# Language-model tower in float32 on one core: parameters loaded as rows, weights held back, the square of the FP4 rounding on ScalarE, and new step lists

## The chip, the cores and the metric

The kernel runs on one core of one Trainium2 chip. The metric is the device time of one execution in microseconds (us). The engines are TensorE (PE in the profile, its weight loads PEld), VectorE (DVE), ScalarE (ACT), GpSimd (POOL) and SyncE (SP). Each engine runs its own list of instructions in order and waits on semaphores.

## What is computed

16 sequences of 256 token ids (4096 tokens) pass through three blocks in float32: an embedding with a projection, one RWKV layer, and a gated feed-forward block whose inputs and weights are rounded to FP4 in blocks of 16.

```python
h = (w0[ids] @ w1) * mask * 16                        # 512 -> 256
x = layernorm(h)                                      # RWKV layer, T = 256
a = ln1(x); ax = shift(a)
k, v, r = mix_k(a, ax) @ wk, mix_v(a, ax) @ wv, sigmoid(mix_r(a, ax) @ wr)
x = x + (r * wkv_scan(k, v, time_decay, time_first)) @ wo
b = ln2(x); bx = shift(b)
x = x + sigmoid(mix_r(b, bx) @ cwr) * (relu(mix_k(b, bx) @ cwk) ** 2 @ cwv)
h = h + x
c = layernorm(h)                                      # FP4 feed-forward, 704 wide
g, u = q(c) @ q(w_gate).T, q(c) @ q(w_up).T
h = h + q(silu(g) * u) @ q(w_down).T
# q: scale = max|block of 16| / 6, then round |x| / scale to 0, .5, 1, 1.5, 2, 3, 4, 6
```

## The kernel before

The tokens are cut into 8 chunks of 512 (four tiles of 128, two sequences). Each chunk passes three stages: `a` (gather of embedding rows by GpSimd, transpose, projection, layer norm, mixes, k, v, r, and the scans and exponentials of the wkv), `b` (output projection, second layer norm, channel mix with the squared ReLU), and `c` (third norm, quantisation, gate and up products, quantisation of the 704-wide product tile by tile, down product, store). Up to three chunks are in flight at once.

What runs when is written out by hand. `ORDER` holds for each engine one list of steps `(name, lag)`; `walk` goes through it once for each t and calls the step for chunk t - lag, where that chunk exists. Steps whose name begins with `w` prepare weights and run once, for chunk 0. So the order on an engine is fixed, and an instruction that waits holds everything behind it. Between engines there are semaphores that count up (`Signal`); the PSUM areas of each stage (`A_JOBS`, `B_JOBS`, `C_JOBS`) have two slots each, and TensorE may write a slot only when the job before last in it was emptied (`wait_free`).

The steps that matter here: `c_norm0/1` on VectorE quantise the normed input (512 columns, two tiles at once), `c_quant0` to `c_quant3` the product tile (704 columns), `w_quant0` to `w_quant2` the weights gate, up and down, in two halves. All call `quantise`, which has nine stages, each waiting for the one before. Stage 0 is the maximum of each block, 1 and 2 scale and reciprocal, 3 divides. Then a magic number rounds: stage 4 masks the exponent out of the value, 5 forms max(exponent, 1) times `MAGIC`, 6 adds it, 7 subtracts it, 8 multiplies by the scale. `w_turn` transposes a quantised weight on TensorE, ScalarE copies the high part, `w_split` on VectorE forms the low part; `w_key` does the same for `cwk` (a copy on ScalarE, a subtraction on VectorE). The gate, up and key products use float32r matmuls and are split in three: high by high, high by low, low by high (`up`, `key` on TensorE).

At the start, SyncE issues the loads of the ids and `tok_w1` and then all weights, wk, wv, wr, gate, up, down, cwk, wo, cwr, cwv. ScalarE issues eleven loads of the parameter vectors, one value per partition (`v.rearrange("(h p) -> p h")`), and waits for all before it forms exp(time_decay); VectorE waits for that before its first list step:

```python
            act.wait_ge(s_par, 16 * len(PARAMS))
            nc.scalar.activation(decay[:, 0], par[:, td, :], ACT.Exp).then_inc(s_exp, 1)
            ...
            dve.wait_ge(s_exp, 1)
            nc.vector.tensor_scalar(decay[:, 1], decay[:, 0], -1.0, None, ALU.mult).then_inc(s_decay, 1)
```

Lines of the profile: L349, L351, L353, L355 are stages 0 to 3 of `quantise`, L358 and L360 stages 4 and 5, L362, L364 and L366 stages 6 to 8. L917 is a mix on VectorE, L730 its part on ScalarE, L955 the scan for the running maximum, L942 and L984 the products and sums of the wkv, L776 its exponentials. L811 and L814 are the ReLU and the square of the keys, L845 the SiLU, L782 the norm of stage b, L803 the copy in `w_key`. On TensorE L487 transposes the gathered rows, L499 is the embedding product, L527 k, v and r, L536 the products of stage b and `b_out`, L562 the keys, L604 gate and up, L631 down.

## Time and profile before

| | |
|---|---|
| median of 3 runs | 795.42 us (795.3 to 796.78) |
| the profiled execution | 792.87 us, span 791.0 us |
| mean granted clock of TensorE | 0.962 of full speed |
| TensorE busy, 3310 matmuls | 705.7 us (89%) |
| TensorE weight loads | 566.1 us (72%) |
| VectorE busy | 651.3 us (82%) |
| ScalarE busy | 473.9 us (60%) |
| GpSimd busy | 155.9 us (20%) |
| DMA over the span | 19.33 MB, mean 24 GB/s |
| chain that ended last, by engine | VectorE 45%, TensorE 30%, ScalarE 11%, issue 10% |

The span runs from the first to the last instruction; the execution's own time is a little longer. Busy times are unions of an engine's instructions. Two matmuls in flight overlap, and their ends are modelled, so start-to-start distances tell more of them than their lengths. The chain is followed back from the last instruction, at each step to whatever released it.

### The profile page before, as it was taken

Reading aid. Unit: us, or ns where it says so; the run is one execution under the profiler, and the core shown is the slowest. Engines: PE = TensorE matmul, PEld = TensorE weight load, DVE = VectorE, ACT = ScalarE, POOL = GpSimd, SP = SyncE. Lnnn points to the kernel's source line nnn. Section 1 sums busy time; section 2 is a strip of 40 time slices with the busy share of each in tenths; the row PEclk is TensorE's granted clock in tenths of the full one; section 3 lists DMA queues with packets and bytes.
Section 4 is the critical chain, followed back from the end, with each engine's and each line's share of the span. In section 5 each row is a group of like instructions: output and inputs, shape, how many; then the busy total and the mean of one; then the engine's idle time right before and its main releaser. Section 6 shows DMA issues by size and latency. Waiting matters only on the chain.

```text
span 791.0 us, 9857 instructions
## 1 busy us (share of the span) xinstructions
PE 705.7 (89%) x3310; PEld 566.1 (72%) x3310; DVE 651.3 (82%) x1131; ACT 473.9 (60%) x834; POOL 155.9 (20%) x220
## 2 busy tenths in 40 slices
PE   2563779899999999999999999999999999699687
PEld 2431656688688867887788868886788778688575
DVE  2987497899799987899789979998889969982874
ACT  1239388568665668377756866676837684561110
POOL 2213230324023401331032402340232003100000
PEclk9867899999999999999999999999999999999978
DMA  8400000000010001000010101000100000000000
GB/s 198 165 27 14 14 27 0 28 1 28 0 41 14 28 1 38 17 1 28 14 41 1 29 0 41 14 28 0 41 15 1 1 14 14 1 0 15 14 0 27
DMA packets 14903, 19.33 MB, mean 24 GB/s; under 512 B 3942, under 2 KB 12294, under 8 KB 14854
## 3 DMA queue, kind: packets, MB, share of 16 engines
q1 hardware_dynamic: 9302, 10.31, 4.3%
q0 software_dynamic: 2560, 8.39, 3.5%
q8 instruction: 27, 0.44, 0.2%
q10 hardware_dynamic: 2992, 0.01, 0.2%
q14 instruction: 22, 0.18, 0.1%
HBM read 14.51 MB, written 4.19 MB: 24 GB/s over the span
## 4 chain that ended last, share of the span: by engine, by line
DVE 45%; PE 30%; ACT 11%; issue 10%; DMA 2%; POOL 2%; DVEq 0%; ACTq 0%; POOLq 0%
PE psB L536 16%; PE psC L631 6%; DVE mix L917 5%; DVE top L349 4%; DVE hq L362 3%; DVE hq L364 3%; DVE hq L355 3%; DVE hq L1096 3%; DVE magic L360 2%; DVE magic L358 2%; DVE top L353 2%; DMA rows<-L_tok_w,ids_now 2%; ACT take L776 2%; PE psB L562 2%; PE psC L604 2%
## 5 line engine op out<-in xcount | busy, mean ns | idle before, releaser
L536 PE MATMUL psB<-cwv_s,kkT 128*128 128x256 f32 x512 | 113.9, 380 | 2.6 <-ACT kkT L814 2.6
L536 PEld LDWEIGHTS psB<-cwv_s,kkT 128*128 128x128 f32 x512 | 96.0, 190 | 20.8 <-ACT kkT L814 8.4
L527 PE MATMUL psA<-mix,kvr_s 128*128 128x512 f32 x192 | 91.4, 622 | 12.8 <-DVE mix L917 10.5
L604 PE MATMUL psC<-up_hi,xq_hi 128*128 128x352 f32 x256 | 89.8, 351 | 13.0 <-DVE xq_lo L1144 12.7
L631 PE MATMUL psC<-downT,hqT 128*128 128x256 f32 (+1 forms) x384 | 95.9, 395 | 0.0
L424 POOL DMA_INDIRECT rows<-L_tok_w,ids_now x32 | 38.6, 1207 | 270.1 <-PE psA L487 258.5
L631 PEld LDWEIGHTS psC<-downT,hqT 128*128 128x128 f32 (+1 forms) x384 | 69.6, 191 | 23.8 <-issue 15.9
L604 PE MATMUL psC<-up_lo,xq_hi 128*128 128x352 f32 x256 | 84.3, 329 | 0.0
L604 PE MATMUL psC<-up_hi,xq_lo 128*128 128x352 f32 x256 | 84.1, 328 | 0.0
L527 PEld LDWEIGHTS psA<-mix,kvr_s 128*128 128x128 f32 x192 | 36.7, 198 | 54.0 <-issue 40.8
L604 PEld LDWEIGHTS psC<-up_hi,xq_hi 128*128 128x128 f32 x256 | 49.6, 194 | 16.9 <-DVE xq_lo L1144 15.5
L499 PE MATMUL psA<-w_s,rowsT 128*128 128x256 f32 x256 | 60.8, 393 | 0.2 <-ACT rowsT L685 0.2
L917 DVE SCALAR_TENSOR_TENSOR mix<-hT,rest,mix 128x512 f32<-128x512 f32 x80 | 54.3, 743 | 7.8 <-ACT mix L730 7.8
L562 PE MATMUL psB<-key_hi,cwk_hi 128*128 128x512 f32 x128 | 56.9, 444 | 0.4 <-ACT rr L821 0.4
L499 PEld LDWEIGHTS psA<-w_s,rowsT 128*128 128x128 f32 x256 | 50.2, 199 | 7.6 <-ACT rowsT L685 0.5
L730 ACT ACTIVATE mix<-hT,par 128x512 f32<-128x512 f32 x80 | 50.9, 715 | 1.1
L837 ACT CAST xq_hi<-psC 128x512 fp32r<-128x512 f32 x16 | 9.4, 585 | 70.3 <-PE psC L590 70.3
L562 PE MATMUL psB<-key_hi,cwk_lo 128*128 128x512 f32 x128 | 50.6, 395 | 0.0
L562 PE MATMUL psB<-key_lo,cwk_hi 128*128 128x512 f32 x128 | 50.6, 395 | 0.0
L604 PEld LDWEIGHTS psC<-up_lo,xq_hi 128*128 128x128 f32 x256 | 49.6, 194 | 0.5
L604 PEld LDWEIGHTS psC<-up_hi,xq_lo 128*128 128x128 f32 x256 | 49.5, 193 | 0.0
L811 ACT ACTIVATE kkT<-psB 128x512 f32<-128x512 f32 x64 | 36.2, 590 | 17.9 <-PE psB L562 17.9
(156 smaller groups left out, 1479.8 us busy)
## 6 DMA issues: line engine op xcount, KB each, us to landing
out<-h SPq DMA_DIRECT2D x16, 256.0 KB, 2.1
mix<-L_attn_cwk SPq DMA_DIRECT2D x1, 1024.0 KB, 16.0
cwv_s<-L_attn_cwv SPq DMA_DIRECT2D x1, 1024.0 KB, 15.7
kkT<-L_ffn_w_gate SPq DMA_DIRECT2D x1, 704.0 KB
kkT<-L_ffn_w_up SPq DMA_DIRECT2D x1, 704.0 KB
hqT<-L_ffn_w_down SPq DMA_DIRECT2D x1, 704.0 KB, 17.1
w_s<-L_tok_w SPq DMA_DIRECT2D x1, 512.0 KB, 4.2
rows<-L_tok_w,ids_now POOLq DMA_INDIRECT x32, 4.2
```

The costliest lines, as they stand in the source:

```text
L349: op = nc.vector.tensor_reduce(big, blocks(data, nb), AX_X, ALU.max, apply_absolute_value=True)
L355: op = nc.vector.scalar_tensor_tensor(out=blocks(data, nb), in0=blocks(data, nb), scalar=NUDGE, in1=wide(big, p, nb), op0=ALU.mult, op1=AL ...
L424: pool.indirect_dma_start(rows[:, q, :], None, tok_w0, bass.IndirectOffsetOnAxis(ap=ids_now[:, s, t:t + 1], axis=0)).then_inc(rows_in[q], 16)
L499: mm = nc.tensor.matmul(psA[:, A.slot(f"e{j}"), q * D:(q + 1) * D], rowsT[:, q, k, :], w1_s[:, k, :], start=(k == 0), stop=(k == KE - 1))
L527: mm = nc.tensor.matmul(psA[:, A.slot(f"{name}{d}")], kvr_s[:, w, k, d * P:(d + 1) * P], mix[:, w, k].rearrange("p c t -> p (c t)"), start ...
L536: mm = nc.tensor.matmul(psB[:, B.slot(name), q * D:(q + 1) * D], lhsT[:, k, (2 * j + q) * P:(2 * j + q + 1) * P], weight[:, k, :], start=( ...
L562: mm = nc.tensor.matmul(psB[:, B.slot(f"kk{m}")], a[:, k, m * P:(m + 1) * P], b[:, k], start=(k == 0 and p == 0), stop=(k == H - 1 and p = ...
L604: mm = nc.tensor.matmul(psC[:, C.slot(name), f, 0:INTER // 2], a[:, k, t * P:(t + 1) * P], b[:, w, k, f * (INTER // 2):(f + 1) * (INTER // ...
L631: mm = nc.tensor.matmul(psC[:, C.slot(name), 0, q * D:(q + 1) * D], hqT[0:n, q, k, :], downT[0:n, k, :], start=(k == 0), stop=(k == KI - 1))
L730: nc.scalar.activation(dst[:, w, d], src[:, d, :, 1:ROW], ACT.Identity, scale=col(m, d)).then_inc(sig.sem, 1)
L811: nc.scalar.activation(kkT[:, m, :], psB[:, B.slot(f"kk{m}")], ACT.Relu).then_inc(b_act.sem, 1)
L917: nc.vector.scalar_tensor_tensor(out=dst[:, w, d], in0=src[:, d, :, 0:T], scalar=rest[:, PARAMS.index(m) - MIXES, d:d + 1], in1=dst[:, w, ...
```

## The change

Five things are changed together.

1. `quantise` has seven stages. The two stages that formed the exponent go. In their place ScalarE forms the square (`square`, float32r) of the value that stage 3 left, scaled by `SPREAD`; the new stage 4 is value + (square + `MAGIC`), stage 5 is (square + `MAGIC`) - value, stage 6 multiplies by minus the scale. Stage 4 waits for the square. ScalarE has nine kinds of steps for it: `c_sqn0/1`, `c_sq0` to `c_sq3`, `w_sq0` to `w_sq2`.
2. The parameters are loaded as 22 rows of 128 values (`par_rows`), TensorE transposes them, VectorE copies them to `par` (`w_par` on three engines). The waits for them at the start of ScalarE and VectorE are gone.
3. SyncE waits for both gathers of the first pair before it issues the weights.
4. `ORDER` has new lists.
5. The three products are taken in the order high by high, low by high, high by low.

```diff
-EXPONENT = 0x7F800000
-MAGIC = 1.5 * 2.0**22
+SPREAD = (2.0**22 / 6.0)**0.5
+MAGIC = 5461.0 * 2.0**10
...
-    "pe": [("c_up0", 2), ("a_turn1", 0), ("c_cols1", 2), ("b_cols", 1), ("a_emb1", 0), ("c_up1", 2), ("c_turn0", 2),
-        ("b_gate", 1), ("c_up2", 2), ("b_key0", 1), ("a_cols", 0), ("b_key1", 1), ("c_turn1", 2), ("w_turn0", 0),
-        ("c_up3", 2), ("w_turn1", 1), ("a_k", 0), ("b_key2", 1), ("a_v", 0), ("b_key3", 1), ("c_down0", 2),
-        ("w_turn2", 1), ("c_turn2", 2), ("a_r", 0), ("b_value0", 1), ("a_turn0", -1), ("c_turn3", 2),
-        ("b_value1", 1), ("c_down1", 2), ("b_out0", 0), ("c_cols0", 1), ("b_out1", 0), ("a_emb0", -1)],
-    "act": [("c_norm0", 2), ("c_cols0", 2), ("c_norm1", 2), ("a_emb0", 0), ("c_up0", 2), ("b_norm", 1),
-        ("a_turn1", 0), ("c_cols1", 2), ("b_cols", 1), ("b_part", 1), ("c_up1", 2), ("a_emb1", 0), ("b_high", 1),
-        ("b_gate", 1), ("c_turn0", 2), ("c_up2", 2), ("a_norm", 0), ("b_key0", 1), ("a_cols", 0), ("c_turn1", 2),
-        ("a_part", 0), ("c_up3", 2), ("b_key1", 1), ("a_k", 0), ("w_turn1", 1), ("w_turn0", 0), ("b_key2", 1),
-        ("a_wkv1", 0), ("a_v", 0), ("a_wkv2", 0), ("w_key", 0), ("b_key3", 1), ("a_r", 0), ("a_wkv3", 0),
-        ("c_turn2", 2), ("a_y", 0), ("c_turn3", 2), ("a_turn0", -1), ("w_turn2", 1)],
+    "pe": [("c_down0", 3), ("a_r", 1), ("b_value0", 2), ("w_par", -1), ("c_turn2", 3), ("c_turn3", 3),
+        ("a_turn0", 0), ("b_value1", 2), ("c_down1", 3), ("b_out0", 1), ("c_cols0", 2), ("b_out1", 1), ("a_emb0", 0),
+        ("c_up0", 2), ("c_cols1", 2), ("a_turn1", 0), ("w_turn1", 1), ("b_cols", 1), ("a_emb1", 0), ("c_up1", 2),
+        ("c_turn0", 2), ("b_gate", 1), ("c_up2", 2), ("b_key0", 1), ("a_cols", 0), ("c_turn1", 2), ("b_key1", 1),
+        ("c_up3", 2), ("w_turn2", 1), ("b_key2", 1), ("w_turn0", 0), ("a_k", 0), ("b_key3", 1), ("a_v", 0)],
+    "act": [("c_cols1", 1), ("b_part", 0), ("w_sq0", -1), ("c_up1", 1), ("a_emb1", -1), ("b_high", 0),
+        ("w_turn1", 0), ("c_turn0", 1), ("b_gate", 0), ("w_sq1", -1), ("c_sq1", 1), ("a_norm", -1), ("c_up2", 1),
+        ("b_key0", 0), ("c_turn1", 1), ("a_cols", -1), ("c_sq2", 1), ("b_key1", 0), ("a_part", -1), ("w_par", -2),
+        ("c_up3", 1), ("b_key2", 0), ("w_key", -1), ("a_k", -1), ("c_sq3", 1), ("b_key3", 0), ("a_v", -1),
+        ("a_wkv1", -1), ("a_wkv2", -1), ("a_r", -1), ("a_wkv3", -1), ("c_turn2", 1), ("w_turn2", 0), ("a_y", -1),
+        ("c_turn3", 1), ("c_norm0", 0), ("a_turn0", -2), ("c_sqn0", 0), ("w_turn0", -1), ("c_cols0", 0),
+        ("c_norm1", 0), ("a_emb0", -2), ("w_sq2", -1), ("c_sqn1", 0), ("c_up0", 0), ("b_norm", -1), ("a_turn1", -2),
+        ("c_sq0", 0), ("b_cols", -1)],
...
                     elif stage == 4:
-                        op = nc.vector.tensor_scalar(w.bitcast(I32), data.bitcast(I32), EXPONENT, None, ALU.bitwise_and)
+                        dve.wait_ge(squared[0], squared[1](k + 1))
+                        op = nc.vector.scalar_tensor_tensor(out=data, in0=w.bitcast(F32), scalar=MAGIC, in1=data,
+                                                            op0=ALU.add, op1=ALU.add)
                     elif stage == 5:
-                        op = nc.vector.tensor_scalar(w, w, 1.0, MAGIC, ALU.max, ALU.mult)
-                    elif stage == 6:
-                        op = nc.vector.tensor_tensor(data, data, w, ALU.add)
-                    elif stage == 7:
-                        op = nc.vector.tensor_tensor(data, data, w, ALU.subtract)
+                        op = nc.vector.scalar_tensor_tensor(out=data, in0=w.bitcast(F32), scalar=MAGIC, in1=data,
+                                                            op0=ALU.add, op1=ALU.subtract)
                     else:
-                        op = nc.vector.tensor_tensor(blocks(data, nb), blocks(data, nb), wide(scale, p, nb), ALU.mult)
+                        op = nc.vector.scalar_tensor_tensor(out=blocks(data, nb), in0=blocks(data, nb), scalar=-1.0,
+                                                            in1=wide(scale, p, nb), op0=ALU.mult, op1=ALU.mult)
...
+            for q in range(2):
+                sp.wait_ge(rows_in[q], 16)
             for k, w in enumerate((wk, wv, wr)):
...
+            def parameters(_):
+                pe.wait_ge(s_par, 16 * len(PARAMS))
+                nc.tensor.transpose(psB[:, 0, 0:len(PARAMS) * H], par_rows[:], ident[0:len(PARAMS) * H, 0:len(PARAMS) * H]
+                                    ).then_inc(s_turned, 1)
...
-                            for p, (a, b) in enumerate(((cwk_hi, key_hi), (cwk_hi, key_lo), (cwk_lo, key_hi))):
+                            for p, (a, b) in enumerate(((cwk_hi, key_hi), (cwk_lo, key_hi), (cwk_hi, key_lo))):
...
-                                for p, (a, b) in enumerate(((xq_hi, up_hi), (xq_hi, up_lo), (xq_lo, up_hi))):
+                                for p, (a, b) in enumerate(((xq_hi, up_hi), (xq_lo, up_hi), (xq_hi, up_lo))):
...
-                    act.dma_start(par[:, k, :], v.rearrange("(h p) -> p h", p=P)).then_inc(s_par, 16)
-            act.wait_ge(s_par, 16 * len(PARAMS))
-            td = PARAMS.index("time_decay")
-            nc.scalar.activation(decay[:, 0], par[:, td, :], ACT.Exp).then_inc(s_exp, 1)
-            act.wait_ge(s_pad, 5)
+            for k, v in enumerate(params):
+                act.dma_start(par_rows[H * k:H * (k + 1), :], v.rearrange("(h p) -> h p", p=P)).then_inc(s_par, 16)
...
+            def square_up(t):
+                def step(ch):
+                    at(act, quant, ch, QUANT * (t + 2) + 4)
+                    nc.scalar.activation(square[:], hq[:, t], ACT.Square, scale=SPREAD).then_inc(squared.sem, 1)
+                return step
+
+            def square_of_w(k):
+                def step(_):
+                    for n in range(2):
+                        act.wait_ge(s_wq, 2 * QUANT * k + 6 + n + 1)
...
+                        nc.scalar.activation(dst, src, ACT.Square, scale=SPREAD).then_inc(s_sq, 1)
```

VectorE's list in a period differs from the old one in two places: `c_down0` now stands before `a_wkv2` and not after it, and `a_stat` before `c_up1`. For the weights it is now `w_par`, `w_quant0`, `a_stat`, `w_quant1`, `a_mix`, `a_wkv1`, `w_key`, the rest of the wkv, `w_split0`, `b_x1`, `w_quant2`, `b_mix`, `a_stat` of chunk 1, `b_low`, `w_split1`, `a_mix` of chunk 1. Before, `w_key` came after `a_wkv3` and `w_quant2` between `b_low` and `a_mix` of chunk 1. GpSimd's list is in the same order as before.

## Rows read from the trace of the kernel before

**Rows 1.** Windows of the span: us, busy us of each engine, granted clock, DMA

```profile
34.00:133.55 99.55, 64.64 (x245) 42.94 (x245) 74.44 (x123) 66.24 (x111) 26.33 (x29) 0.83 0.05 16
...
303.24:388.55 85.31, 84.36 (x408) 68.28 (x408) 75.35 (x135) 58.46 (x104) 19.25 (x26) 1.00 0.06 19
...
559.20:644.52 85.32, 84.35 (x408) 68.29 (x408) 75.36 (x135) 58.47 (x104) 16.26 (x22) 1.00 0.04 13
```

**Rows 2.** What TensorE waited for from 303.24 to 388.55: us, times, longest

```profile
PE psC L604 <- DVE xq_lo L1144: 0.6, 1, 0.6
PE psB L536 <- ACT kkT L814: 0.3, 1, 0.3
```

**Rows 3.** What VectorE waited for, same period

```profile
DVE takev L942 <- ACT take L776: 5.3, 1, 5.3
```

**Rows 4.** Timeline of TensorE, same period: start us, us, instruction

```profile
332.16 0.32 PE L604 MATMUL psC<-up_lo,xq_hi 128*128 128x352 f32 x1
...
335.67 0.32 PE L604 MATMUL psC<-up_hi,xq_lo 128*128 128x352 f32 x1
```

**Rows 5.** Timeline of VectorE, same period, stages 4 to 6 of `c_quant1`

```profile
353.04 0.53 DVE L358 TENSOR_SCALAR magic<-hq 128x704 int32<-128x704 int32 x1
353.60 0.53 DVE L360 TENSOR_SCALAR magic<-magic 128x704 f32<-128x704 f32 x1
354.16 0.89 DVE L362 TENSOR_TENSOR hq<-hq,magic 128x704 f32<-128x704 f32 x1
```

**Rows 6.** Groups of instructions by line: busy us, mean ns, idle before

```profile
L814 ACT ACTIVATE kkT<-kkT 128x512 f32<-128x512 f32 x64 | 36.6, 625 | 0.0
...
L803 ACT CAST cwk_hi<-mix 128x2048 fp32r<-128x2048 f32 x1 | 1.9, 1886 | 0.0
```

**Rows 7.** Timeline of ScalarE, same period, `c_up2`

```profile
352.25 1.28 ACT L845 ACT_TABLE_LOAD   x1
353.54 0.77 ACT L845 ACTIVATE hq<-psC 128x704 f32<-128x704 f32 x1
```

**Rows 8.** Timeline of the start, all engines

```profile
15.63 1.12 PE L487 MATMUL psA<-ident,rows 128*128 128x128 f32 x4 [0.23 <-DMA rows<-L_tok_w,ids_now]
...
16.32 0.17 DVE L899 TENSOR_SCALAR decay<-decay 128x2 f32<-128x2 f32 x1 [11.82 <-ACT decay L675]
...
16.60 2.34 DVE L349 TENSOR_REDUCE hq<-kkT 88x64 f32<-88x1024 f32 x2
...
22.17 1.28 DVE L358 TENSOR_SCALAR hq<-kkT 88x1024 int32<-88x1024 int32 x2
...
24.58 2.35 DVE L362 TENSOR_TENSOR kkT<-kkT,hq 88x1024 f32<-88x1024 f32 x2
...
34.14 2.31 DVE L349 TENSOR_REDUCE hq<-kkT 88x64 f32<-88x1024 f32 x2
...
48.90 4.05 DVE L917 SCALAR_TENSOR_TENSOR mix<-hT,rest,mix 128x512 f32<-128x512 f32 x6
```

**Rows 9.** Landing of the gathers, and GB/s in the span's 40 slices

```profile
DMA to landing us min/median/max: 4.0/4.2/8.2
...
GB/s 198 165 27 14 14 27 0 28 1 28 0 41 14 28 1 38 17 1 28 14 41 1 29 0 41 14 28 0 41 15 1 1 14 14 1 0 15 14 0 27
```

**Rows 10.** Timeline around chunk 0's second half and chunk 1's start

```profile
92.63 2.07 ACT L782 ACTIVATE mix<-mix,sc_b 128x256 f32<-128x256 f32 x4 [0.63 <-POOL sc_b L437]
...
97.87 2.74 DVE L917 SCALAR_TENSOR_TENSOR mix<-hT,rest,mix 128x512 f32<-128x512 f32 x4 [7.75 <-ACT mix L730]
...
103.39 1.67 DVE L349 TENSOR_REDUCE hq<-hqT 128x44 f32<-128x704 f32 x2
...
113.92 4.05 DVE L917 SCALAR_TENSOR_TENSOR mix<-hT,rest,mix 128x512 f32<-128x512 f32 x6
...
130.03 1.29 DVE L942 TENSOR_TENSOR takev<-take,vT 128x512 f32<-128x512 f32 x2 [5.45 <-ACT take L776]
...
133.55 7.17 PE L536 MATMUL psB<-cwv_s,kkT 128*128 128x256 f32 x32 [0.71 <-ACT kkT L814]
```

84 lines of the change are left out of this document (55 added, 29 removed), and 10 rows, old and new, of the table ORDER.

## The prediction

> **What bounds the kernel now.** I first cut the span into windows and looked for a pattern. From 217.93 us to 644.52 us it repeats every 85.3 us, one period per chunk, five times; rows 1 show the second and the last. In a period TensorE is busy 84.36 us, VectorE 75.35 and ScalarE 58.46, at a granted clock of 1.00 [rows 1]. The waits of TensorE in that window are two, 0.6 us for `xq_lo` and 0.3 us for the squared `kkT` [rows 2]. So in the middle of the kernel TensorE is nearly never idle: whatever VectorE saves there can return at most about 0.95 us a period. VectorE has one large wait, 5.3 us for the exponentials [rows 3]. The chain of waits nevertheless runs through VectorE for most of a period, then through ScalarE's exponentials and key squares to `b_value0`, so the engines are balanced and a lateness anywhere shows soon.
>
> Busy matmul time overlaps, so I checked the spacing: the matmuls of 352 columns of one tile start 0.16 us apart (22 distances from the second to the last of 24, 3.51 us), each drawn as 0.32 us [rows 4]. 352 columns at 2.4 GHz are 0.147 us, so there is no hidden gap worth more than a tenth. The Trainium skill (Perfetto Trace Analysis, Identifying the Most-Contended Engine) calls matmul busy share a poor measure and points to the share of weight loads, here 68.28 of 85.31 us, 80%. By that rule there would be 20% of headroom; it is a rival below.
>
> The other 360 us are the start and the end. From 34 to 133.55 us TensorE is busy 64.64 of 99.55 us at a mean clock of 0.83 [rows 1]: this is where time can be had.
>
> **The change, part by part.**
>
> *Square from ScalarE.* Stages 4 and 5 (`and`, `max` with product) go, from 353.04 to 354.16 = 1.12 us on a 704 tile [rows 5]; the three remaining wide stages keep two inputs and so their 0.89 us. In exchange VectorE must wait after stage 3 for one Square on ScalarE. The trace has a Square of 512 columns at 0.625 us and a copy of 2048 at 1.886 us [rows 6], thus 0.82 ns a column, 0.78 us for 704; with some 0.1 us for the two hand-overs the wait is 0.89 us. A 704 quantisation gains 0.2 us if ScalarE is free at that moment, and not the 1.12 us that leave VectorE's busy time. The bound downward is the full 1.12 us if the wait were covered; nothing covers it, since the queue of VectorE is in order and stage 4 is next. The bound upward is set by what ScalarE is doing: in the new list `c_sq1` stands ahead of `a_norm` and `c_up2`. `c_up2` is a table load of 1.28 us and an activation of 0.77 us [rows 7] that could run at 352.25 before. Now ScalarE sits in `c_sq1` until about 354.0, then `a_norm` takes 2.07 us (as the four of rows 10 do), so `c_up2` ends near 358.1, some 3.8 us later. VectorE wants it at 356.9: 1.2 us lost. The same happens once more at `c_sq2`, again 1.2 us by the same reckoning. VectorE's saved 4 x 0.2 and 2 x 0.2 us are smaller than that. It is hidden in a period because VectorE's 5.3 us wait [rows 3] gets shorter and because `c_down0` moves into it; TensorE meets it only at `b_key1`, whose two slots wait for `b_key0` on ScalarE: 0.8 us by my reckoning. If that cover is gone, each microsecond is one on the period.
>
> *The new lists in the period.* `b_key3` now comes before the exponentials on ScalarE, so `b_value0` no longer waits behind them (the 0.3 us of rows 2, and the ScalarE part of the chain). `c_turn1` and the key steps move, `a_k` and `a_v` each swap with a key step, `c_down0` goes before `a_r`. TensorE does the same work. Following it from one `b_value0` to the next I get 84.5 to 84.9 us against 85.31: I take -0.55 us. Bounds: -0.95 us (all idle time of today) and +1 us (one more microsecond of ScalarE's lateness at `b_key1`). Six periods, 133.55 to 644.52: **-3.3 us** (-5.7 to +6).
>
> *The order of the three products.* Both orders load weights for every matmul. In the present order one product of three keeps its stationary operand; a mean distance of 0.16 us over all three kinds [rows 4], with 0.147 as the floor, leaves no room for one of them to be much slower. I take 0. The bound is the 13 ns (9%) over the column time, on 96 of these and 48 of the keys a chunk: at most 2 us a period, which nothing in the trace supports.
>
> *Parameters in rows, weights held back.* Eleven loads of single 4-byte values now hold ScalarE, and through `decay` VectorE: it waits 11.82 us and starts `w_quant0` at 16.60 [rows 8]. With rows that gate is gone. A gather takes up to 8.2 us to land, the median 4.2 [rows 9]; the slow ones are those that share the queues with the weights. The second gather of chunk 0 was there at 15.63 [rows 8], so it left at 7.4 and will be there at 11.6. But what VectorE does first is `w_quant0`, and its weights now leave only at 11.7. They and the three projection weights ahead of them (704 x 256 and 3 x 256 x 256 floats) are 1472 KB; at the 198 GB/s of the first slice [rows 9] 7.6 us, so 19.3 us at the earliest. With the second pair of gathers (512 KB) ahead of them and at the 165 GB/s of the second slice it is 12.3 us: 24 at the latest. I take 21, so VectorE starts 4.4 us **later** than now. A weight takes 14.8 us (`w_quant1`, 34.14 to 48.90); two stages in two halves, 22.17 to 24.58, are gone (2.41 us) [rows 8], and the Square of one half (1024 columns, 1.04 us) is hidden under the other half's 1.14 us. So: 21 + 12.4 = 33.4, `a_stat` to 35.0 (34.1 before), `w_quant1` to 47.4, `a_mix` of chunk 0 at 47.5 against 48.90. On ScalarE `w_sq1` holds `a_norm` some 5 us, covered by VectorE being in `w_quant1` meanwhile. **-1.4 us** (-3.1 to +1.6). The second pair of gathers comes about 4 us sooner too, but `h0` then waits for VectorE: nothing.
>
> *The weight steps after that.* `w_key` leaves the exponentials (its copy of 1.89 us [rows 6] runs while ScalarE waits for `a_k`) and `a_v` goes before them: net -1.2 us at `b_out` of chunk 0. The clock there may recover sooner since TensorE pauses less before `a_k`: up to -2.5, I count -0.6. `w_quant2` stood ahead of `a_mix` of chunk 1, 103.39 to 113.92 = 10.5 us; it moves into the hole of 7.75 us at 97.87 [rows 10]. This looks like 8 us won, and isn't: `w_sq2` stands ahead of `b_norm`. That began at 92.63, 2.5 us after VectorE went idle at 97.87 - 7.75 = 90.1; it will begin some 5.2 us after, since stages 0 to 3 of `w_quant2` (1.7 us for each wide one, 1 for the small ones) and a square come first: +2.7. And `b_key1` (2.2 us, four activations of rows 6) with `w_turn1` goes ahead of `a_part` of chunk 1. With the 3.2 us won so far, `a_mix` of chunk 1 comes at 113.7 against 113.92. TensorE gains 4 us there by doing `b_key2` in its wait, but must then wait for VectorE: the exponentials of chunk 1 now stand behind `a_v`, so `takev` moves from 130.03 to 131.3, and what VectorE does with the first `b_value0` (TensorE: 133.55), for which it waited, stays where it is. The whole start is thus worth **-1 us** (-6 if TensorE's 4 us and the clock survive, +4 if the weights come at 24).
>
> *The end.* The last chunk's six quantisations follow each other on VectorE with ScalarE idle: 6 x 0.2 = 1.3 us. `b_value0` stands ahead of `c_turn2`, 0.6 us. **-1.9 us** (-3 to 0).
>
> **The sum**, against the profiled execution of 792.87 us (span 791.0): -1 - 3.3 - 1.9 = -6.2, hence 786.7 us. The median of the runs is 2.55 us above it, so 795.42 - 6.2 = **789.2 us**. About 0.2% (1.6 us) can be told from no change.
>
> **The rivals.**
> *A, as summed*, 789.2, own range 785.5 to 793.8: chance 0.45.
> *B, the start keeps its gains*: TensorE's 4 us and the clock reach the first period. For: TensorE is idle 35 of those 99.55 us. Against: VectorE is the chain there. 789.2 - 5 = 784: chance 0.15.
> *C, only the end remains*: one wait of TensorE takes the place of another (0.95 us a period stays) and `w_sq2` eats the start: 795.4 - 1.3 = 794.1: chance 0.2.
> *D, ScalarE is late (slower)*. Place: `b_key1`, behind `c_sq1`, `a_norm`, `c_up2` and `b_key0` in one queue. Price: if TensorE waits there 1.8 us and not 0.8, the period grows by 0.5 us; with another 0.3 at `c_up3` behind `c_sq2` by 0.8 us, six times 5, less 2 from start and end: 798.4. It decides from about 1.9 us of TensorE waits in a period. For: six new two-way rendezvous a chunk. Against: ScalarE goes only from 58.5 to some 63 us busy of 85. Chance 0.17.
> *E, headroom in TensorE*: were the matmuls loosely packed, the period would be VectorE's: 75.35 less the two stages (4 x 1.12 + 2 x 0.9), plus 5.4 for the squares and some 6 of the other waits, 80.5 us, or 29 us less in six: 766. The spacing of 0.16 us speaks against it. It is what the weight-load share of the page named above would allow. Chance 0.03.
>
> **How the numbers follow.** Faster: A nearly whole (0.43), B, E and a little of C: 0.64. Same: most of C, the upper edge of A: 0.19. Slower: 0.17. The range from B to the lower half of D: 782.5 to 797.5.
>
> **What would show it.** Right: in a period windows with VectorE busy near 69 us and ScalarE near 63, a wait of some 0.9 us of VectorE for `square` six times, two of them near 2 us; a period of 84.5 to 84.9; TensorE waiting for the `kkT` evacuation; `w_quant0` starting at 21 us and `a_mix` at 47.5; matmuls of 352 columns still 0.16 us apart. Wrong: a period over 85.3 (D) or under 84.2; weights landing at another time, by which the whole start slides; a first `b_value0` before 130 us with VectorE following (B); a change in matmul spacing, which would speak for the order of the products.

## The result

The changed kernel takes **789.66 us**, the median of 5 executions (788.11 to 790.58), against 795.3 us (793.49 to 796.78, 5 executions). The ratio is 0.9936, with a 95% interval of 0.9919 to 0.9954: faster by 0.64%, 5.6 us. The forecast was 789.2 us. One execution of the experiments, of the kernel with the square in the old lists, took 1786.5 us against 823 to 828 of its five others; the ratios leave it out.

That the number was met doesn't say that each step was. The profiled executions are 792.87 us before and 790.58 us after, spans of 791.0 and 788.8: they differ by 2.2 us, not by 5.6. The profiled execution of before was faster than any of its five, that of after the slowest of its own. I come back to this below, where the end is told.

Windows of the changed kernel, same columns as [rows 1]: the start up to the first `b_value0`, and two periods.

```profile
34.00:133.06 99.06, 62.00 (x244) 43.72 (x245) 71.68 (x118) 65.78 (x108) 23.74 (x29) 0.79 0.08 25
388.71:473.14 84.43, 83.85 (x409) 68.46 (x408) 69.83 (x122) 62.59 (x110) 17.86 (x26) 1.00 0.06 20
557.58:642.01 84.43, 83.85 (x409) 68.47 (x408) 69.83 (x122) 62.58 (x110) 14.54 (x22) 1.00 0.04 13
```

A period has fallen from 85.32 to 84.43 us. VectorE gave up 5.5 us of work (75.35 to 69.83), ScalarE took 4.1 (58.46 to 62.59), and TensorE is busy 83.85 of 84.43 us, so 0.6 us of a period is left. The chain that ended last says the same. This is its share by engine; before it read 45% VectorE, 30% TensorE.

```profile
PE 69%; DVE 15%; ACT 7%; issue 6%; DMA 2%; POOL 0%; SPq 0%; DVEq 0%; ACTq 0%; POOLq 0%
```

What TensorE waited for from 388.71 to 473.14 us (to set beside [rows 2]), and then VectorE in the same period (beside [rows 3]): us, times, longest.

```profile
PE psC L601 <- DVE normc L368: 0.3, 1, 0.3
PE psB L519 <- ACT mix L796: 0.2, 1, 0.2
```

```profile
DVE hq L362 <- ACT square L873: 4.2, 4, 1.4
DVE h L1161 <- PE psC L642: 3.1, 1, 3.1
DVE normc L362 <- ACT square L866: 1.5, 2, 0.8
DVE top L352 <- ACT normc L843: 1.4, 1, 1.4
DVE hq L1145 <- ACT hq L859: 1.3, 1, 1.3
DVE xq_lo L1194 <- ACT xq_hi L851: 1.0, 1, 1.0
DVE takev L988 <- ACT take L790: 0.5, 1, 0.5
```

Neither the squared `kkT` nor `xq_lo` holds TensorE any more. VectorE's 5.3 us wait for the exponentials is down to 0.5; six waits for the square, 5.7 us in all, have taken its place, and they cost next to nothing, since the two waits of TensorE that are left come to 0.5 us.

One quantisation of the hidden tile, VectorE's timeline (beside [rows 5]), and ScalarE's in the same place (beside [rows 7]); start us, us, instruction.

```profile
353.32 0.89 DVE L358 SCALAR_TENSOR_TENSOR hq<-hq,top 128x704 f32<-128x704 f32 x1
355.15 0.89 DVE L362 SCALAR_TENSOR_TENSOR hq<-square,hq 128x704 f32<-128x704 f32 x1 [0.94 <-ACT square L873]
356.07 0.89 DVE L365 SCALAR_TENSOR_TENSOR hq<-square,hq 128x704 f32<-128x704 f32 x1
357.00 0.89 DVE L368 SCALAR_TENSOR_TENSOR hq<-hq,top 128x704 f32<-128x704 f32 x1
359.18 0.89 DVE L1145 TENSOR_TENSOR hq<-psC,hq 128x704 f32<-128x704 f32 x1 [1.29 <-ACT hq L859]
```

```profile
354.24 0.79 ACT L873 ACTIVATE square<-hq 128x704 fp32r<-128x704 f32 x1 [1.31 <-DVE hq L358]
354.94 2.07 ACT L721 ACTIVATE kT<-h,sc_a 128x256 f32<-128x256 f32 x4
357.03 1.28 ACT L859 ACT_TABLE_LOAD   x1
358.32 0.76 ACT L859 ACTIVATE hq<-psC 128x704 f32<-128x704 f32 x1
```

The square takes 0.79 us and VectorE stands still for 0.94 us around it; right after, `c_up2` ends at 359.08 on ScalarE and VectorE waits 1.29 us for it. The Trainium skill (ScalarE: Activation LUTs, What ACT_TABLE_LOAD costs) gives 186 ns and 0.833 ns a column for an activation with immediate scale and bias, an estimate of 772 ns for these 704 columns. The trace agrees: 0.79 us.

The start (beside [rows 8]), VectorE's timeline:

```profile
24.76 2.35 DVE L352 TENSOR_REDUCE hq<-kkT 88x64 f32<-88x1024 f32 x2 [17.51 <-DMA kkT<-L_ffn_w_gate]
30.47 1.22 DVE L362 SCALAR_TENSOR_TENSOR kkT<-xq_hi,kkT 88x1024 f32<-88x1024 f32 x1
38.93 2.31 DVE L352 TENSOR_REDUCE hq<-kkT 88x64 f32<-88x1024 f32 x2
51.43 4.05 DVE L963 SCALAR_TENSOR_TENSOR mix<-hT,rest,mix 128x512 f32<-128x512 f32 x6
```

The gate weight is there at 24.76 us, VectorE had waited 17.51 us for it, and the first mixing starts later than before (51.43 against 48.90). And where that lateness comes out, timelines of VectorE and TensorE (beside [rows 10]):

```profile
118.34 4.07 DVE L963 SCALAR_TENSOR_TENSOR mix<-hT,rest,mix 128x512 f32<-128x512 f32 x6 [8.81 <-ACT mix L744]
135.95 1.29 DVE L988 TENSOR_TENSOR takev<-take,vT 128x512 f32<-128x512 f32 x2 [7.65 <-ACT take L790]
```

```profile
133.06 7.07 PE L546 MATMUL psB<-cwv_s,kkT 128*128 128x256 f32 x32
153.23 3.75 PE L546 MATMUL psB<-wo_s,rT 128*128 128x256 f32 x8 [5.32 <-DVE rT L985]
```

`b_value0` of chunk 0 starts as early as before (133.06, before 133.55), but `takev` of chunk 1 is 5.9 us later, and 20 us further on TensorE waits 5.32 us for `rT` at `b_out0` of chunk 1. The lateness is there before that: the mixing of chunk 1 starts at 118.34, before at 113.92. Not all of the 5.32 us is new, for before TensorE stood in the same place for the normed input:

```profile
153.96 0.66 PE L590 MATMUL psC<-ident,normc 128*128 128x128 f32 x4 [3.71 <-DVE normc L366]
```

All waits of TensorE in the first period come to 7.5 us, before to 5.2. So it is 86.63 us long, 2.25 us more than the 84.38 before.

The table below is read from TensorE's timeline, where each `b_value0` starts; the mean period is over the five from the second to the seventh start. It has the experiments too, since most of what they tell is in it. The times are those of the profiled executions, but for the median; the last column is the span, as the page rounds it, less the eighth start.

| kernel | median us | gate weight used | 1st | 2nd | mean period | 8th | 8th to the end |
|---|---|---|---|---|---|---|---|
| before | 795.3 | 16.60 | 133.55 | 217.93 | 85.32 | 717.07 | 73.9 |
| changed | 789.66 | 24.76 | 133.06 | 219.69 | 84.46 | 714.01 | 74.8 |
| changed, again | 788.9 | 23.69 | 133.35 | 219.99 | 84.48 | 714.38 | 74.7 |
| weights not held | 789.83 | 14.56 | 133.55 | 220.20 | 84.47 | 714.55 | 72.7 |
| gate, up first, held | 786.14 | 18.88 | 131.05 | 217.70 | 84.47 | 712.05 | 72.6 |
| gate, up before the wait | 791.18 | 11.64 | 133.03 | 219.66 | 84.48 | 714.04 | 71.8 |
| old product order | 789.07 | 24.30 | 133.16 | 219.81 | 84.47 | 714.14 | 71.8 |
| new lists, no square | 797.78 | 24.77 | 138.82 | 226.18 | 84.54 | 722.60 | 72.9 |
| square in the old lists | 825.24 | 16.80 | 141.61 | 229.00 | 88.87 | 751.10 | 72.3 |
| `b_key3` late | 803.88 | 24.46 | 139.16 | 225.94 | 85.84 | 727.23 | 72.6 |
| square in the old lists, moved | 800.1 | 16.94 | 142.60 | 226.10 | 85.13 | 726.15 | 72.1 |
| gate, up first, square early | 787.97 | 18.77 | 130.58 | 217.23 | 84.48 | 711.62 | 74.8 |
| gate alone first, square early | 783.28 | 11.45 | 126.42 | 213.09 | 84.47 | 707.45 | 71.7 |
| columns again | 790.39 | 23.69 | 133.47 | 220.12 | 84.51 | 715.00 | 74.2 |

The experiments ran in three groups of four: the table's rows from "changed, again" to "gate, up before the wait", from "old product order" to "`b_key3` late", and the rest. Beside them before had medians of 794.07, 795.21 and 794.98 us, and each ratio below is to the one of its group, so medians of different groups compare only to about 1 us.

### The profile page after: what moved, and what is told of

Read it like the earlier page. It is cut to its first block, busy times and chain, and to the rows that moved or that the text cites. A ratio compares the mean times of both kernels' runs of the same rounds, so it can differ in the third digit from the quotient of the medians.

```text
span 788.8 us, 9882 instructions
## 1 busy us (share of the span) xinstructions
PE 698.7 (89%) x3311; PEld 566.1 (72%) x3311; DVE 600.1 (76%) x1023; ACT 511.7 (65%) x889; POOL 147.8 (19%) x220
## 4 chain that ended last, share of the span: by engine, by line
PE 69%; DVE 15%; ACT 7%; issue 6%; DMA 2%; POOL 0%; SPq 0%; DVEq 0%; ACTq 0%; POOLq 0%
PE psB L546 17%; PE psB L573 11%; PE psC L642 11%; PE psC L615 11%; PE psA L537 9%; PE psA L509 3%; PE psC L629 3%; ACT mix L796 2%; DMA kkT<-L_ffn_w_gate 2%; DVE top L352 1%; DVE mix L1082 1%; PE psB L519 1%; PE psA L519 1%; DVE top L949 1%; ACT take L790 1%
## 5 line engine op out<-in xcount | busy, mean ns | idle before, releaser
L429 POOL DMA_INDIRECT rows<-L_tok_w,ids_now x32 | 45.7, 1427 | 266.7 <-PE psA L497 255.1
L642 PEld LDWEIGHTS psC<-downT,hqT 128*128 128x128 f32 (+1 forms) x384 | 70.2, 193 | 26.7 <-issue 19.0
L537 PE MATMUL psA<-mix,kvr_s 128*128 128x512 f32 x192 | 86.8, 596 | 1.5 <-DVE mix L963 1.3
L615 PEld LDWEIGHTS psC<-up_hi,xq_hi 128*128 128x128 f32 x256 | 49.3, 193 | 10.1 <-DVE xq_lo L1194 8.0
L573 PE MATMUL psB<-key_hi,cwk_hi 128*128 128x512 f32 x128 | 54.3, 424 | 1.9 <-ACT rr L835 1.9
L362 DVE SCALAR_TENSOR_TENSOR hq<-square,hq 128x704 f32<-128x704 f32 x32 | 28.6, 893 | 35.1 <-ACT square L873 35.1
L546 PE MATMUL psB<-wo_s,rT 128*128 128x256 f32 x128 | 34.1, 415 | 17.1 <-DVE rT L985 17.1
```

Source lines behind the costliest of these rows:

```text
L362: op = nc.vector.scalar_tensor_tensor(out=data, in0=w.bitcast(F32), scalar=MAGIC, in1=data, op0=ALU.add, op1=ALU.add)
L429: pool.indirect_dma_start(rows[:, q, :], None, tok_w0, bass.IndirectOffsetOnAxis(ap=ids_now[:, s, t:t + 1], axis=0)).then_inc(rows_in[q], 16)
L537: mm = nc.tensor.matmul(psA[:, A.slot(f"{name}{d}")], kvr_s[:, w, k, d * P:(d + 1) * P], mix[:, w, k].rearrange("p c t -> p (c t)"), start ...
L546: mm = nc.tensor.matmul(psB[:, B.slot(name), q * D:(q + 1) * D], lhsT[:, k, (2 * j + q) * P:(2 * j + q + 1) * P], weight[:, k, :], start=( ...
L573: mm = nc.tensor.matmul(psB[:, B.slot(f"kk{m}")], a[:, k, m * P:(m + 1) * P], b[:, k], start=(k == 0 and p == 0), stop=(k == H - 1 and p = ...
L615: mm = nc.tensor.matmul(psC[:, C.slot(name), f, 0:INTER // 2], a[:, k, t * P:(t + 1) * P], b[:, w, k, f * (INTER // 2):(f + 1) * (INTER // ...
```

## The experiments

**The start: what is it waiting for?** My reading was that it lost time since the gate weight landed at 24.8 us and not at 21. Four kernels, of which the first is the control, the changed kernel unchanged.

> The changed kernel once more, unchanged, as the control for the three that run beside it. Both theories: 789.7 us, 0.9936 of before (0.992 to 0.9955); the gate weight lands at 24 to 25 us and the period is 84.4 to 84.5 us.

Measured: 788.9 us (786.06 to 791.03), ratio to before 0.9928 (0.9904 to 0.9951).

Weights not held back:

```diff
-            for q in range(2):
-                sp.wait_ge(rows_in[q], 16)
```

> SyncE's two waits for the first gathers are taken out, so all weights are issued from about 2 us on. Theory (the start lost time because the gate weight landed at 24.8 us and not at 21): the first gathers land 3 to 5 us later (13.5 to 15), the gate weight 3 to 5 us sooner (20 to 22), the first mix ends 2 to 4 us sooner, 787 us, 1 to 3 below the control. Rival (the held weights are what the start needs, or the start is bound by the gathers): the start is no shorter, 789 to 791 us. The period is 84.4 in both.

Gate and up first, behind the wait:

```diff
             for q in range(2):
                 sp.wait_ge(rows_in[q], 16)
-            for k, w in enumerate((wk, wv, wr)):
-                sp.dma_start(kvr_s[:, k], ...)
             for k, w in enumerate((w_gate, w_up)):
                 sp.dma_start(raw_up[:, k * GJ:(k + 1) * GJ, :], ...)
+            for k, w in enumerate((wk, wv, wr)):
+                sp.dma_start(kvr_s[:, k], ...)
```

> Weights still held back until the first gathers are in, but gate and up are issued ahead of wk, wv and wr. Theory (the gate weight is late because three transfers are queued before it): it lands at 15 to 18 us, the first mix ends 5 to 7 us sooner than the control, and the time is 785 us (783 to 788). Rival (VectorE's quantisation of the weights is not on the path of the start): under 1 us off the control.

Gate and up first and ahead of the wait:

```diff
+            for k, w in enumerate((w_gate, w_up)):
+                sp.dma_start(raw_up[:, k * GJ:(k + 1) * GJ, :], ...)
             for q in range(2):
                 sp.wait_ge(rows_in[q], 16)
             for k, w in enumerate((wk, wv, wr)):
                 sp.dma_start(kvr_s[:, k], ...)
-            for k, w in enumerate((w_gate, w_up)):
-                sp.dma_start(raw_up[:, k * GJ:(k + 1) * GJ, :], ...)
```

> Gate and up are issued before the wait for the gathers, the other weights after it. Theory: the gate weight lands at 12 to 15 us, the first gathers 1 to 3 us later than in the control, the first quantisation starts 8 to 11 us sooner than in the control and the time is 784 us (782 to 788). Rival (the start is bound by the gathers): no gain over the control, or 1 us more, as the gathers come later.

Measured: without the hold 789.83 us (ratio 0.9943, 0.9923 to 0.9964); gate and up first 786.14 (0.9903, 0.9883 to 0.9922); ahead of the wait 791.18 (0.9964, 0.9946 to 0.9982). The gate weight did come 9.1, 4.8 and 12.1 us before the control's 23.69, and only the middle one gained, 2.8 us against the control and 2.3 at the first `b_value0`. So the theory holds for one of three, and the rival for two. None of the landing times that I expected for the gate weight was met: 14.56 and not 20 to 22, 18.88 and not 15 to 18, 11.64 and not 12 to 15, and in the control 23.69 and not 24 to 25. The 791.18 us of the last are the median of twelve executions; its row of the table is from the fastest of them (787.61), and there too its first and eighth `b_value0` are within 0.4 us of the control's. What it had left out stands in VectorE's timeline, first without the hold, then with gate and up ahead of the wait:

```profile
17.92 2.29 DVE L358 SCALAR_TENSOR_TENSOR kkT<-kkT,hq 88x1024 f32<-88x1024 f32 x2
28.60 1.22 DVE L362 SCALAR_TENSOR_TENSOR kkT<-xq_hi,kkT 88x1024 f32<-88x1024 f32 x1 [8.40 <-ACT xq_hi L883]
```

```profile
15.00 2.29 DVE L358 SCALAR_TENSOR_TENSOR kkT<-kkT,hq 88x1024 f32<-88x1024 f32 x2
29.89 1.22 DVE L362 SCALAR_TENSOR_TENSOR kkT<-xq_hi,kkT 88x1024 f32<-88x1024 f32 x1 [12.60 <-ACT xq_hi L885]
```

VectorE is through stage 3 of the gate weight and then waits 8.4 and 12.6 us for its square. `w_sq0` stands behind `a_turn1` in ScalarE's list, thus behind the second pair of gathers (landed at 26.27 and 27.09 us in these two, at about 24.8 in the changed kernel). In the changed kernel nobody sees this, because the gate weight is later still: its stage 4 follows stage 3 at once (28.12 and 30.47 above). Two things bound the start, one just behind the other.

**Taking both away.** `w_sq0` is moved forward in ScalarE's list:

```diff
-    "act": [("c_cols1", 1), ("b_part", 0), ("w_sq0", -1), ("c_up1", 1), ...
+    "act": [("c_cols1", 1), ("b_part", 0), ("c_up1", 1), ...
-        ... ("b_norm", -1), ("a_turn1", -2),
+        ... ("b_norm", -1), ("w_sq0", -2), ("a_turn1", -2),
```

with gate and up first behind the wait as above:

> Gate and up issued first after the wait for the gathers, and ScalarE's square of the gate weight one step earlier, in front of its copy of the second pair of gathered tiles. Theory (with the gate weight at 18.9 us the square stands behind the second gather and costs 1.6 us): the wait for the square falls to 1.0 us, the first mix is done 0.5 to 1 us sooner than with gate and up first alone, 785.5 us (784.5 to 787). Rival (moving it in front makes the gathered tiles late instead): same as gate and up first alone, 786 us, or 1 us more.

And in front of `a_emb0`, with the gate weight alone ahead of SyncE's wait:

```diff
-        ("c_norm1", 0), ("a_emb0", -2), ...
+        ("c_norm1", 0), ("w_sq0", -2), ("a_emb0", -2), ...
...
+            sp.dma_start(raw_up[:, 0:GJ, :], ...).then_inc(s_raw[0], 16)
             for q in range(2):
                 sp.wait_ge(rows_in[q], 16)
+            sp.dma_start(raw_up[:, GJ:2 * GJ, :], ...).then_inc(s_raw[1], 16)
             for k, w in enumerate((wk, wv, wr)):
```

> The gate weight alone is issued before the wait for the gathers, up, wk, wv and wr after it, and the square of the gate weight stands in front of the first embedding step on ScalarE. Theory (what kept the kernel with gate and up ahead of the wait from gaining was the square behind the second gather, 12.6 us, and gathers that came 4 us later): gate at 10 to 12 us, its square at 17 us, statistics at 30 to 32 us, first mix at 44 to 46 us against 51.4 in the changed kernel and 47.1 with gate and up first, 784.5 us (783 to 786.5). Rival (the gathers are late again with one transfer ahead of them): first mix at 48 us or later, 787 us or more.

Measured: 787.97 us (784.54 to 788.2), ratio 0.9897 (0.9871 to 0.9923), for the first: no gain over gate and up first alone (0.9903, 0.9883 to 0.9922). Its VectorE goes through the square without a wait, and then:

```profile
24.48 1.22 DVE L362 SCALAR_TENSOR_TENSOR kkT<-xq_hi,kkT 88x1024 f32<-88x1024 f32 x1
33.51 1.41 DVE L949 BATCH_NORM_STATS2 top<-h 128x6 f32<-128x256 f32 x4 [2.13 <-ACT h L712]
47.66 4.06 DVE L963 SCALAR_TENSOR_TENSOR mix<-hT,rest,mix 128x512 f32<-128x512 f32 x6
```

The wait of 1.61 us for the square has turned into one of 2.13 us for the embedded tiles, whose copies now stand behind the square: its rival was right. Up to the eighth `b_value0` its profile is 0.4 us ahead of that of gate and up first alone; the 2.2 us by which its end is longer are told of below.

The second is **783.28 us** (781.01 to 783.96), ratio 0.9854 (0.9831 to 0.9876): the best of all, 6.4 us under the changed kernel (6.5 by the ratios). Its VectorE:

```profile
11.45 2.34 DVE L352 TENSOR_REDUCE hq<-kkT 88x64 f32<-88x1024 f32 x2 [1.83 <-DMA kkT<-L_ffn_w_gate]
17.16 1.22 DVE L362 SCALAR_TENSOR_TENSOR kkT<-xq_hi,kkT 88x1024 f32<-88x1024 f32 x1
30.16 1.41 DVE L949 BATCH_NORM_STATS2 top<-h 128x6 f32<-128x256 f32 x4 [6.04 <-ACT h L712]
44.32 4.05 DVE L963 SCALAR_TENSOR_TENSOR mix<-hT,rest,mix 128x512 f32<-128x512 f32 x6
```

The first mixing starts 7.1 us sooner than in the changed kernel, the first `b_value0` 6.6 us (126.42), every later one the same 6.6 us: what the start wins here is kept to the end. All of its expected times were met. VectorE now waits 6.04 us for the second pair of gathers and their embedding. Which of the two did it, the gate weight alone ahead of the wait or its square ahead of `a_emb0`, wasn't separated.

**Parameters in columns again**, in the changed kernel:

```diff
-                act.dma_start(par_rows[H * k:H * (k + 1), :], v.rearrange("(h p) -> h p", p=P)).then_inc(s_par, 16)
+                act.dma_start(par[:, k, :], v.rearrange("(h p) -> p h", p=P)).then_inc(s_par, 16)
```

(TensorE's transposition and VectorE's copy of them go too.)

> The changed kernel with the parameters read as columns again (2,816 single values instead of 22 rows), copied and turned by nobody. Theory (the small packets stand ahead of the gathers and of all that is held back behind them): first gathers 2 to 4 us later, gate weight at 27 to 29 us, start 2 to 4 us longer, 791 to 794 us. Rival (the parameters were hidden behind the gate weight's transfer anyway): within 1 us of the changed kernel, 789 to 790.5 us.

Measured: 790.39 us (787.53 to 792.38), ratio 0.9944 (0.9924 to 0.9964), which overlaps the changed kernel's. The theory was wrong and the rival right. The columns were complete when VectorE read them at 8.21 us:

```profile
8.21 0.18 DVE L938 TENSOR_SCALAR rest<-par 128x14 f32<-128x14 f32 x1 [3.66 <-DMA par<-L_attn_cm_mix_r]
```

and the first gathers landed at 10.04 and 11.52 us, as with rows (9.78 and 11.25). Without the hold, rows and all, they came at 14.66. So it is the hold that brought the first gathers forward, the second of them from 15.63 [rows 8] to 11.25; beside it the rows did nothing that shows. Where the weights aren't held, VectorE starts on the gate weight at 14.56 us with rows and at 16.80 and 16.94 with columns (the two kernels with the old lists below). The queue of the parameters went from 2992 packets to 44, and the small packets cost time only in the kernels whose weights were issued beside them.

**The middle: lists or square?** Four kernels.

```diff
-                            for p, (a, b) in enumerate(((cwk_hi, key_hi), (cwk_lo, key_hi), (cwk_hi, key_lo))):
+                            for p, (a, b) in enumerate(((cwk_hi, key_hi), (cwk_hi, key_lo), (cwk_lo, key_hi))):
...
-                                for p, (a, b) in enumerate(((xq_hi, up_hi), (xq_lo, up_hi), (xq_hi, up_lo))):
+                                for p, (a, b) in enumerate(((xq_hi, up_hi), (xq_hi, up_lo), (xq_lo, up_hi))):
```

> The changed kernel with the three products in their old order. Theory (the order is worth nothing: the spacing of the matmuls is the same): 789.7 us, within 1 us of the changed kernel, period 84.4 us. Rival (the order gave the 0.5 us by which TensorE's busy time of a period fell): period 84.9 to 85.0 us, 793 us.

Measured: 789.07 us, ratio 0.9931 (0.9911 to 0.9951), mean period 84.47. The product order is worth nothing that shows, as the theory had it. The spacing says so too; TensorE's timeline in the changed kernel, second and last of the 24 matmuls of a tile (beside [rows 4]):

```profile
418.18 0.32 PE L615 MATMUL psC<-up_hi,xq_lo 128*128 128x352 f32 x1
...
421.69 0.32 PE L615 MATMUL psC<-up_lo,xq_hi 128*128 128x352 f32 x1
```

3.51 us, as before.

The new lists with the nine stages of before and no square:

```diff
-QUANT = 7
+QUANT = 9
...
-                        dve.wait_ge(squared[0], squared[1](k + 1))
-                        op = nc.vector.scalar_tensor_tensor(out=data, in0=w.bitcast(F32), scalar=MAGIC, in1=data, ...
+                        op = nc.vector.tensor_scalar(w.bitcast(I32), data.bitcast(I32), EXPONENT, None, ALU.bitwise_and)
...
```

and the steps `c_sqn0`, `c_sqn1`, `c_sq0` to `c_sq3` and `w_sq0` to `w_sq2` taken out of ScalarE's list.

> The new lists with the quantisation of the kernel before (nine stages on VectorE, no square on ScalarE). Theory (in the middle the order of the steps gives most, as TensorE is near its bound once VectorE is off the path): VectorE has 5.5 us more to do per period, of which 69.9 + 5.5 = 75.4 still fits in 84.4; period 84.6 to 85.3 us, end 1 to 2 us longer, start 2 us longer, 791 to 797 us. Rival (the square gave the gain): period 85.3 us or more, 797 us or more, since the new lists are made for the shorter quantisation.

Measured: 797.78 us, ratio 1.0039 (1.0024 to 1.0054): **slower than before**. Yet its period is 84.54 us. Its window of one period:

```profile
395.27:479.80 84.53, 83.94 (x410) 68.42 (x409) 75.45 (x134) 59.22 (x104) 18.14 (x26) 1.00 0.06 19
```

VectorE has all its old work (75.45 us) and the period is shorter by 0.79 all the same: that gain belongs to the lists. What it loses is for the most part in the start: its first mixing starts at 55.95 us, since two weights of 14.75 us follow a gate weight that lands at 24.77, and its second `b_value0` is at 226.18, 8.25 us after the one of before and 6.5 after that of the changed kernel. From the seventh to the eighth it takes 73.7 us, before 72.55 and the changed kernel 72.00. The time is 0.8 us above what the theory gave and within the rival's; the period, 84.54 and not 85.3 or more, is against the rival.

The square with the old lists, nothing else changed; each square behind the step that it needs, the third as follows:

```diff
-        ... ("b_key0", 1), ("a_cols", 0), ("c_turn1", 2), ("a_part", 0), ...
+        ... ("b_key0", 1), ("a_cols", 0), ("c_turn1", 2), ("w_sq1", 0), ("c_sq2", 2), ("a_part", 0), ...
```

> The kernel before with the quantisation through the square alone (seven stages, the squares put into ScalarE's old list each behind the step that it needs), columns of parameters, old product order, weights not held back. Theory (the old lists keep the key product's eviction behind the exponentials, so TensorE still waits there): period 84.9 to 85.4 us, end 1.2 us shorter, 792 to 795 us. Rival (the square alone carries the gain): period 84.4 us, 788 to 791 us. If a square stands badly in the old list: slower than before, 797 us or more.

Measured: 825.24 us, ratio 1.0377 (1.0351 to 1.0403), period 88.87. `c_sq2` stood behind `c_turn1`, which waits for TensorE, and VectorE for it:

```profile
468.04 0.89 DVE L360 SCALAR_TENSOR_TENSOR hq<-square,hq 128x704 f32<-128x704 f32 x1 [4.24 <-ACT square L860]
```

The theory's 792 to 795 was missed and its warning of a badly placed square came true. So this told more of the price of one than of the square. Again with `c_sq2` right behind `b_key0`:

```diff
-        ... ("b_key0", 1), ("a_cols", 0), ("c_turn1", 2), ("w_sq1", 0), ("c_sq2", 2), ("a_part", 0), ...
+        ... ("b_key0", 1), ("c_sq2", 2), ("a_cols", 0), ("c_turn1", 2), ("w_sq1", 0), ("a_part", 0), ...
```

> The kernel before with the square alone once more, the third hidden tile's square now in front of ScalarE's copy of the mixing columns and of the turned hidden tile, and not behind them, so that it doesn't wait for TensorE. Theory (the square in the old lists only pays once its place is right, and even then the eviction of the last key product behind the exponentials keeps TensorE waiting): the 4.2 us wait for that square falls to 1 to 2 us, period 85.5 to 87 us, 798 to 808 us. Rival (the square alone carries the gain): period 84.9 us or less, under 792 us.

Measured: 800.1 us, ratio 1.0064 (1.0041 to 1.0088), mean period 85.13. VectorE's waits in one of its periods, 396.55 to 481.52:

```profile
DVE takev L969 <- ACT take L777: 5.2, 1, 5.2
DVE hq L360 <- ACT square L860: 3.7, 4, 0.9
```

The wait for the exponentials is what it was (5.2 against 5.3 [rows 3]): with the old lists the freed time of VectorE turns into waits for the square, and 0.2 us a period remain. The wait for the third square fell from 4.2 us to 0.9 at most. The period is shorter than I expected (85.5 to 87), and the kernel is slower than before only by its start (second `b_value0` 8.2 us later), where the gate weight's square came after 10.1 us of waiting.

`b_key3` on ScalarE back behind two steps of exponentials:

```diff
-        ... ("c_sq3", 1), ("b_key3", 0), ("a_v", -1), ("a_wkv1", -1), ("a_wkv2", -1), ("a_r", -1), ...
+        ... ("c_sq3", 1), ("a_v", -1), ("a_wkv1", -1), ("a_wkv2", -1), ("b_key3", 0), ("a_r", -1), ...
```

> The changed kernel with one step moved in ScalarE's list: the eviction of the last key product stands behind the first two steps of exponentials again, as before. Theory (that move took the wait for kkT off the path): the wait of the value product comes back, 0.5 to 2 us per period, 793 to 800 us. Rival (another move or the square did it): within 1.5 us of the changed kernel.

Measured: 803.88 us, ratio 1.0108 (1.0086 to 1.0131), mean period 85.84, 1.4 us more than in the changed kernel. TensorE's largest wait in one period, 397.73 to 483.52:

```profile
PE psB L546 <- ACT kkT L828: 1.1, 1, 1.1
```

The wait for the squared `kkT` is back at `b_value0`, larger than in [rows 2]; the whole is 14 us (11.0 between the two profiles) and more than the 10 us that I expected at most. That one move is worth more than the whole gain of a period, and the start lost 6.1 us by it as well (139.16 against 133.06).

## Why the prediction was right, and where it wasn't

Counted as the prediction cut it, on the profiled executions: up to the first `b_value0` -0.5 us (forecast -1), the six periods -2.0 (-3.3), the rest +0.3 (-1.9): -2.2 in sum, where -6.2 was forecast. So the medians agree with the forecast better than its terms do.

- **The period**: right in mechanism, too small in size. 84.46 us against "84.5 to 84.9", -0.86 and not -0.55 a period. The wait at `b_key1` that I charged 0.8 us didn't come at all; the waits of TensorE in a period come to 0.5 us together. That refutes rival D, and rival C's period too. The order of the steps gives 0.78 of the 0.86 (new lists, no square), and `b_key3` ahead of the exponentials is a step without which it is lost. One thing was overlooked: the first of the six periods was 84.38 us long in before already, as long as the others are now, so the gain could be had five times and not six.
- **The square**: 0.94 us of waiting for 704 columns (0.89 forecast), 0.79 us on ScalarE (0.78), VectorE 69.8 us a period (69), ScalarE 62.6 (63), and 1.29 us at `c_up2` (1.2). The second long wait, after `c_sq2`, didn't come, nor were two of the six waits for the square near 2 us: the longest is 1.4. In the middle it is worth 0.1 to 0.2 us a period. Its worth is in the start: there VectorE is the path, a weight takes 12.5 us (38.93 to 51.43, forecast 12.4) and not 14.8, and without it the second `b_value0` is 6.5 us later.
- **The order of the three products**: 0, as forecast, 3.51 us for 22 distances in both. Rival E falls with it: TensorE is busy 99% of a period now, and with the square VectorE has 5.6 us less to do in a period than with the new lists alone (69.83 and 75.45) while the period is only 0.1 us shorter. By the share of weight loads, one of two measures in the rule of the Trainium skill that the prediction weighed (Perfetto Trace Analysis, Identifying the Most-Contended Engine), 68.46 of 84.43 us or 81% would still leave a fifth; the trace doesn't agree.
- **The start**: this term failed. Forecast were -1 us up to the first `b_value0` and -0.55 for the period behind it; measured is +1.8 us at the second `b_value0`. Two parts of it. First the landing of the gate weight, "I take 21" between 19.3 and 24: it was 24.76, outside the bound. The bound counted 1984 KB, the three projection weights, the gate and the second pair of gathers. The window from the first weight's issue to the landing (us, busy us of each engine, clock, DMA share, GB/s) shows that the rate wasn't what was wrong with it:

```profile
11.29:24.76 13.47, 6.29 (x24) 4.92 (x24) 0.00 (x1) 1.74 (x5) 1.89 (x2) 0.84 0.88 195
```

195 GB/s lie between the 165 and 198 that it took, but over 13.47 us they are 2.6 MB and not the 2.03 counted: weights issued behind the gate weight, up 0.5 us and down 1.0 us later, moved beside it. The later landing is nearly all of the 3.9 us by which the first mixing missed its forecast (51.43 and 47.5).

Second, the step "what VectorE does with the first `b_value0` stays where it is": it held for `b_value0` itself, but the mixing of chunk 1 came at 118.34 and not at 113.7 and `takev` at 135.95 and not at 131.3, and I didn't follow that on to `b_out0` of chunk 1, where TensorE pays 5.32 us.

Gate and up first comes near the start that I forecast, with its first mixing at 47.10: there the second `b_value0` is at 217.70, 0.2 us earlier than in the kernel before, where -1.55 was forecast. So of the 3.3 us by which the term is off, 2.0 are the late weight's and 1.3 the first period's, by this one pair. All kernels with the new lists have a first period of 86.6 us or more, the one with the early gate weight too (126.42 to 213.09), so the late weight isn't the cause of its length.

The long waits in it are for ScalarE (8.81 and 7.65 us above), whose list puts the key steps and `a_v` of chunk 1 first; which of these moves it is was not tried. The -0.6 us counted for a clock that recovers sooner doesn't show: the granted clock from 34 us to the first `b_value0` is 0.79, before 0.83. That the hold delays what VectorE needs first was right in direction, and rows against columns, which I had down as the gate's removal, is worth nothing beside the hold.

- **The square of a weight "hidden"**: true of the gate weight only because it is so late. Had it landed at 21, its stage 3 would have been over at 26.7 and ScalarE through with the second gather at 26.5, as in the changed kernel, so that by an estimate from these times VectorE would have waited about 1 us for the square; at 18.88 it waited 1.61, at 14.56 8.4 us.
- **The end**: I counted 1.9 us for all that follows the seventh `b_value0`. From the seventh `b_value0` (642.01, before 644.52) to the eighth it is 0.55 us less. The three quantisations of the last chunk that follow each other are 7.01 us apart and not 7.24, 0.23 us each as forecast. The rest of the term can't be read from this pair, for the clock differs (below).

**The difference that stays open.** The profiled pair gives -2.2 us, the medians -5.6 (by the interval 3.7 to 6.4). The same last part of the program gives different ends: 71.8 us from the eighth `b_value0` on in two kernels, 72.6 in two more, 74.8 and 74.7 in the two profiles of the changed one. VectorE's last instruction, in the changed kernel and in that with the old product order:

```profile
785.46 0.69 DVE L1161 TENSOR_TENSOR h<-h,psC 128x512 f32<-128x512 f32 x1 [9.44 <-PE psC L642]
```

```profile
782.65 0.69 DVE L1161 TENSOR_TENSOR h<-h,psC 128x512 f32<-128x512 f32 x1 [6.80 <-PE psC L642]
```

9.44 and 6.80 us for the same matmuls before it. Windows of TensorE over their first part:

```profile
774.01:780.01 6.00, 3.85 (x12) 3.33 (x13) 1.97 (x3) 0.99 (x4) 0.00 (x0) 0.56 0.14 46
```

```profile
774.14:780.14 6.00, 4.14 (x21) 3.25 (x22) 1.68 (x3) 0.90 (x3) 0.00 (x0) 1.00 0.14 46
```

At a mean granted clock of 0.56 TensorE is mostly at 1.2 GHz there, at 1.00 it is at 2.4. What it did in the 15 us ahead is nearly the same, 12.03 us busy in the changed kernel and 11.74 in the other. In before this wait was 8.41. With 6.80 in both, the profiled pair would differ by 3.2 us instead of 2.2. The other 2.4 us lie in executions that have no profile, and only one of before has one. Their mean granted clocks are on record and go with their times: of the twelve of gate, up before the wait the three at 0.962 and more took 787.6 to 788.8 us, the five at 0.952 and less 791.7 to 795.5. In before they are 0.955 to 0.965, in the changed kernel and its control 0.948 to 0.962. These are means over a whole execution; whether the changed kernel meets the faster clock more often, in its start or its end, was not shown. So the stages account for about half of the forecast 6.2 us (3.2), and that the number came out so near 789.2 is luck in the other half.
